# One more matmul of constants per group in the first layer of a graph network kernel

## What is computed

```
# layer 0: softmax-weighted sum of messages, then a linear map
m = relu(feat[src]) + EPS
ex = exp(m - segment_max(m, dst)[dst])
msg = segment_sum(ex / segment_sum(ex, dst)[dst] * m, dst)
x = layernorm(x + (feat + msg) @ W + b)
# layer 1: attention over edges, 8 heads of 12
score = exp(clip(sum(K[src] * Q[dst] / sqrt(12) * E), -5, 5))
h = segment_sum(V[src] * score, dst) / (segment_sum(score, dst) + 1e-6)
x = layernorm(x + h)
```

## Time and profile before

| | us |
|---|---|
| median of three runs | 5226.73 |
| lowest and highest run | 5209.57, 5227.79 |
| the profiled execution | 5248.06 |
| its span, first to last instruction | 5246.3 |

### The profile page before, as it was taken

How to read it: one execution, slowest core, us unless ns; L and a number is a source line. 1 busy time by engine, 2 the same in 40 slices (tenths; PEclk the granted TensorE clock), 3 DMA queues, 4 the chain that set the end, 5 groups by cost and what they waited for, 6 DMA issues and landing times.

```text
span 5246.3 us, 52541 instructions
## 1 busy us (share of the span) xinstructions
PE 3084.1 (59%) x16572; PEld 2872.6 (55%) x16572; DVE 1883.1 (36%) x5136; ACT 845.8 (16%) x1933; POOL 3240.7 (62%) x3330
## 2 busy tenths in 40 slices
PE   2445454554454445444566666776667676777776
PEld 2445444444444444444566666665666566666666
DVE  3223222222222222222334444444444444444444
ACT  1212222222222222222201111101101110111111
POOL 6666666666666666666466656666666566666664
PEclk9855555555555555555556666566665656665666
DMA  3111111111111111111133333333333333333333
GB/s 93 37 38 37 42 38 37 36 42 37 37 37 43 37 37 37 43 37 37 46 99 106 103 102 105 104 104 101 106 103 105 99 106 104 103 102 103 106 105 82
DMA packets 277580, 376.85 MB, mean 72 GB/s; under 512 B 140757, under 2 KB 183414, under 8 KB 277302
## 3 DMA queue, kind: packets, MB, share of 16 engines
q0 software_dynamic: 132864, 245.03, 18.2%
q1 hardware_dynamic: 144438, 128.41, 8.5%
HBM read 353.82 MB, written 19.32 MB: 71 GB/s over the span
## 4 chain that ended last, share of the span: by engine, by line
another core or an unknown queue 48%; PE 23%; issue 12%; DVE 9%; ACT 7%; DVEq 0%; ACTq 0%
PE banks L493 6%; PE banks L534 6%; PE banks L523 4%; PE banks L554 3%; ACT ex L633 3%; PE banks L543 3%; ACT relu L626 2%; DVE mt L767 2%; DVE ex L838 1%; DVE prod L902 1%; PE banks L467 1%; DVE score L917 1%; DVE onehot L742 1%; DVE prod L888 1%
## 5 line engine op out<-in xcount | busy, mean ns | idle before, releaser
L405 POOL DMA_INDIRECT rows<-key_value,src_i x1661 | 1625.2, 978 | 1051.8 <-DVE vals L894 517.2
L405 POOL DMA_INDIRECT rows<-in_x,src_i x1661 | 1614.1, 972 | 922.2 <-issue 510.1
L493 PE MATMUL banks<-onehot,ex 128*96 128x64 f32 x6644 | 1074.2, 355 | 1273.6 <-ACT ex L633 713.2
L493 PEld LDWEIGHTS banks<-onehot,ex 128*96 128x96 f32 x6644 | 1039.9, 267 | 1313.6 <-issue 1111.7
L534 PE MATMUL banks<-qw,onehot_t 128*128 128x192 f32 x1664 | 590.5, 503 | 478.4 <-ACT onehot_t L659 378.1
L534 PEld LDWEIGHTS banks<-qw,onehot_t 128*128 128x128 f32 x1664 | 435.1, 299 | 505.2 <-ACT onehot_t L659 399.3
L523 PE MATMUL banks<-we_sb,ea 97*128 97x96 f32 x3322 | 665.5, 366 | 0.3 <-issue 0.3
L523 PEld LDWEIGHTS banks<-we_sb,ea 97*128 97x128 f32 x3322 | 615.6, 276 | 0.0
L848 DVE TENSOR_TENSOR sums<-sums,banks 96x128 f32 x416 | 117.3, 282 | 1343.4 <-remote 1157.7
L554 PEld LDWEIGHTS banks<-onehot,vals 128*104 128x104 f32 x3322 | 575.7, 266 | 1.2 <-DVE vals L894 1.1
L554 PE MATMUL banks<-onehot,vals 128*104 128x64 f32 x3322 | 566.8, 343 | 1.0 <-DVE vals L894 1.0
(11 more groups left out here) (90 smaller groups left out, 1237.9 us busy)
## 6 DMA issues: line engine op xcount, KB each, us to landing
ea<-in_edge_t SPq DMA_DIRECT2D x415, 192.0 KB
rows<-in_x,src_i POOLq DMA_INDIRECT x1661
rows<-key_value,src_i POOLq DMA_INDIRECT x1661
qw<-query SPq DMA_DIRECT2D x832, 24.0 KB
key_value<-qkv SPq DMA_DIRECT2D x24, 384.0 KB
xt<-in_x_t SPq DMA_DIRECT2D x7, 672.0 KB, 11.8
query<-qkv SPq DMA_DIRECT2D x24, 192.0 KB
out<-outs SPq DMA_DIRECT2D x24, 192.0 KB
```

What stands on the lines that cost most here:

```text
L405: pool.indirect_dma_start(out=to[0:n, r, u, :], out_offset=None, in_=table, in_offset=bass.IndirectOffsetOnAxis(ap=src_i[0:n, g * G + u:g ...
L493: last = nc.tensor.matmul(ps_sum0[b][:, j, :], ex[:, b, u, j * D:(j + 1) * D], onehot[:, r, u, :], start=u == 0, stop=u == n - 1)
```

## The change

In the first layer TensorE runs, after each group but the last and after the node stages that follow it, one matmul of the 128x128 identity on 512 columns of `rel`, into PSUM bank 6. Nobody waits for it, it increments no semaphore, and its result is read nowhere. The check of the edge lists gets a tighter limit, RN - WIN - CN instead of RN - WIN.

```diff
         ps_misc = banks[:, 7, :]
+        ps_spare = banks[:, 6, :]
+        spare_rows = rel[:, :, :].rearrange("p a b -> p (a b)")[:, 0:512]
         ps_e = [banks[:, b, 0:G * D] for b in range(2)]
...
+                def keep_running(n):
+                    for _ in range(n):
+                        nc.tensor.matmul(ps_spare, ident[:, :], spare_rows, start=True, stop=True)
+
                 for g in range(NG):
                     sum_rows(g)
                     node_stages(g - 1)
+                    if g + 1 < NG:
+                        keep_running(1)
                 for at in range(NG - 1, NG + 6):
                     node_stages(at)
...
-            V.tensor_scalar(lim[:, 2:3], lim[:, 2:3], float(RN - WIN), None, ALU.is_gt)
+            V.tensor_scalar(lim[:, 2:3], lim[:, 2:3], float(RN - WIN - CN), None, ALU.is_gt)
```

## The result

The changed kernel took 5253.55 us (median of 8 runs, 5242.02 to 5272.07) against 5224.17 us of the kernel before in the same comparison: a ratio of 1.006, with a 95% interval of 1.0044 to 1.0075. That is 29 us more, where 98 us were forecast. The time lies in the range given; the sign is right and the size is less than a third.

A forecast was written before the change was run, and what follows sets the result against it. It took the first layer as bound by gathers at 5.13 us a group plus stalls from late releases. About 100 us on the profiled 5248.06 us gave 5348, the median 21 us lower 5327; forecast 5325 us, range 5190 to 5470.

The forecast's parts named there:

- What bounds it: First layer: gathers at 5.13 us a group plus 5.49 us stalls on the relu, with TensorE's releases coming late.
- The filler's length: The added 512-column matmul on TensorE takes 1.72 us at the low clock, 0.86 us at the high one.
- The clock: TensorE's clock rises after one or two groups worked in a row and falls again before the next stretch; granted about 0.65.
- burst: Stretch of the first layer in which TensorE does several groups' sums without a break, 2.62 us a group before the change.
- The size: Loss in the first layer near 100 us, estimated twice, as 90 us and 107 us.
- The first way: First layer: 5.55 groups to a stall become 4.55, 0.22 us a group more, 90 us over 416 groups.
- cycle: First layer's repeating unit: five or six groups of gathers, then a stall of 5.49 us ending with the next relu.
- the 3.4 us: About 2 x 1.72 us that each unbroken stretch of TensorE's sums pays before the clock has risen.
- The second: Compares both layers: 1.43 us more TensorE work goes with 0.21 us more time, slope 0.15, giving 107 us.
- Hidden: Rival: late releases alone limit the first layer, TensorE's idle time takes the added matmul; 5227 us, chance 0.20.
- Faster: Rival: TensorE's clock rises early and stays up, about 100 us of gain, 5125 us; chance 0.17.
- The last sentence of the prediction: If first-layer gathers keep 6.10 us a group or get faster; faster means releases depend on TensorE's clock or what follows the sum.

The follow-up runs named there:

- narrow filler: Changed kernel with the added matmul on 64 columns instead of 512: 5241.82 us, ratio 1.0043 to the kernel before; on the third slow chip 5247.76 us, ratio 1.0038.
- small matmuls: Changed kernel with eight matmuls of 32 columns and 32-column weights per group instead of one of 512: 5498.14 us (ratio 1.0430); on a fast chip 4334.77 us (0.9984).
- BF16 filler: Changed kernel with the added matmul reading the same bytes as BF16, one weight load and one 512-column pass per group: 5292.15 us, ratio 1.0120 to the kernel before.

## Why the prediction was off

**What bounds it.** Right for the chips it was read on, and said to be unknown: the releases that come late. I took this for a trait of the kernel. It is one of the chip together with the gathers: on two of five chips the same program takes 4343 us, bound by GpSimd's gathers alone, as the traces of its variants there show.

**The filler's length.** Right: 1015.35 - 1013.54 = 1.81 us at the low clock against 1.72, and 1020.11 - 1019.20 = 0.91 us at the high one against 0.86.

**The clock.** Right in what it does: 0.69 in the layer against about 0.65 foreseen, up after one or two groups of a burst (0.96 from 1015.4 to 1022 us), down before the next (0.50 from 1030 to 1040 us). That this gives time back was not shown; the wide and the narrow filler on the third late chip, with and without it, are 3 us apart, each known to some 10 us.

**The size.** This is the step that failed, in both its ways: the filler was priced by TensorE's time. The first way had a cycle lose one group to the 3.4 us, 75 stalls becoming some 90 and the pace 0.22 us a group slower; the trace has 77 stalls and the old pace. The second took a slope from two layers that differ in TensorE's busy time, 0.15 us of pace per us. They differ in instructions too: 44 instructions a group in the second (8 + 8 passes of 64 and 96 columns, 4 of 192 and 2 transposes, each with its weight load), 32 in the first. The 0.21 us between them is 87 us over 416 groups, and 12 instructions at 4.5 to 7.2 us (18 / 4 of the narrow filler to 230 / 32 of the small matmuls) are 54 to 86 us, at the second layer's own 4 us 48 us. So the count can carry half of it or more, and the slope was no price of time alone. The filler is heavy in time, 1.72 us, and light in instructions, 4: by time I got 98 us, by count it is 4 x 4.5 to 4 x 7.2, 18 to 29 us, and 29, 5 and 23 us were measured. That two ways gave about 100 us was no support, as both priced the same quantity. And that the sign and the range came out is in part luck: they were reached by cycles that lose a group, which this trace doesn't show.

**The rivals.** "Hidden" is nearer than the forecast on all three late chips (29, 5 and 23 us against 98), closest on the second, and holds on a prompt chip even for 32 instructions; the changed kernel itself wasn't run on one. "Faster" never came. The last sentence of the prediction, that the releases may depend on what follows the sum, was nearer to the matter than its sum.

What stays open is the mechanism: no run shows what holds TensorE's instructions back. One rival explanation is the transfers of the instruction queue (q8 on the page), since its packets grow with the count: 139 in the kernel before, 143 with the BF16 filler and 191 with the eight small matmuls. Against it: 191 packets on the prompt chip and on the late one alike, some 255 instructions to a packet (32 x 415 / 52), where the late passes start one by one, and 4 packets more that go with 65 us where 52 go with 230. The 191 packets took 0.3% of 16 engines' 4333.0 us on the prompt chip and 0.2% of 5496.6 us on the late one, with the rounding 173 to 243 and 132 to 220 us, so slower transfers on the late chip don't show. And the BF16 filler shows that the count isn't the whole law.

## To carry to other kernels

When waits end "remote" on a single core, look in the timeline for single instructions of TensorE with idle "issue" between them (here 0.7 us or a multiple of it apart): it may then be held to a rate of instructions. Price added work there by count as well as by time, and test it with two fillers of the same count and different time. A slope taken from two stretches prices whatever differs between them, so list all that differs. And where one engine's late releases make the time, compare on more than one chip before a gain or a loss of half a percent is believed.

## What the runs showed of the hardware

- The same program takes 5224 to 5268 us on three chips and 4343 us on two; the difference is in releases from TensorE while GpSimd gathers. With a quarter of the gathers the first layer is equal on both kinds (1111.1 and 1114.1 us).
- On a late chip 16 passes took 14.7 us, starting 0.7 us or a multiple apart (with the eight transposes), and 7.6 us in another run (with the eight small matmuls, 1013.78 - 1006.17); back to back they take 2.6 us at the low clock and 1.3 us at the high one (1019.20 - 1017.87 in the changed kernel).
- With eight FP32 transposes per group, which ran beside the sums, the granted clock of the window was 0.69, as with the filler of 512 columns, against 0.55 in the kernel before.
- In the run with twelve buffers the first layer's window reads a granted clock of 1.00, while its sums take 2.79 us, as those at 989.17 us in the kernel before, where the clock reads 0.50 (989 to 992 us); so the 1.00 can't be the clock that they ran at:

```profile
150.00:2150.00 2000.00, 1251.87 (x6724) 1148.73 (x6724) 594.13 (x1553) 498.18 (x943) 1536.20 (x1523) 1.00 0.20 45
```

```profile
1001.74 2.79 PE L493 MATMUL banks<-onehot,ex 128*96 128x64 f32 x16 [2.45 <-issue]
```
